# A macaron transformer kernel: the routing of its MoE stages done chunk by chunk, their inner values rounded by another engine, and a norm moved to an earlier layer

## The reference, cut to what matters

```python
x = x + 0.5 * ffn(norm(x))        # L0 FFN, first time
x = x + mamba(norm(x))
x = x + 0.5 * ffn(norm(x))        # L0 FFN, second time
x = x + 0.5 * moe(norm(x))        # L1 MoE, first time
x = x + attention(norm(x))        # 32 heads in all, 1024 x 1024 scores each
x = x + 0.5 * moe(norm(x))        # L1 MoE, second time

def ffn(x):                       # 128 -> 512 -> 512 -> 512 -> 128
    h = silu(x @ w1.T * s1) * (x @ w2.T * s2)
    h = gelu(h @ h1.T * sh1); h = gelu(h @ h2.T * sh2)
    return h @ w3.T * s3

def moe(x):                       # 16 experts of 64 inner values, 4 chosen per token, one shared expert
    scores = sigmoid(x @ gate_w.T)
    idx = top_k(scores + gate_b, 4)
    w = scores[idx] / sum(scores[idx]) * 2.5
    comb[token, idx] = w
    y = sum_e comb[:, e] * (silu_and_mul(x @ w13_e.T) @ w2_e.T)
    return y + silu_and_mul(x @ w13_s.T) @ w2_s.T
```

## Time and profile before

| | |
|---|---|
| median of three executions | 2157.31 us |
| the profiled execution | 2159.68 us, span 2158.4 us |
| PE busy | 1964.8 us, 91% of the span |
| DVE busy | 1332.5 us, 62% |
| POOL busy | 1163.6 us, 54% |
| ACT busy | 1081.9 us, 50% |
| mean granted TensorE clock | 0.945 of full speed |

### The profile page before, as it was taken

How to read it: one execution, slowest core, us unless ns; L and a number is a source line. 1 busy time by engine, 2 the same in 40 slices (tenths; PEclk the granted TensorE clock), 3 DMA queues, 4 the chain that set the end, 5 groups by cost and what they waited for, 6 DMA issues and landing times. The chain is left out here.

```text
span 2158.4 us, 21996 instructions
## 1 busy us (share of the span) xinstructions
PE 1964.8 (91%) x7432; PEld 1314.0 (61%) x7432; DVE 1332.5 (62%) x2243; ACT 1081.9 (50%) x1508; POOL 1163.6 (54%) x632
## 2 busy tenths in 40 slices
PE   6997899897998894799999999999999999998499
PEld 4772333332776562577777777777777777775265
DVE  5326778887344763466576666666666666665466
ACT  4327566554334224465565656555565555553421
POOL 2350547653543443157666675766666666668234
PEclk8998799899998996899999999999999999999689
DMA  2000000000001003231313222231313222200100
GB/s 86 1 1 1 0 0 1 0 0 0 1 1 38 0 6 78 62 67 36 72 42 67 46 62 62 46 72 37 72 37 72 46 62 61 45 11 11 43 6 15
DMA packets 45761, 73.80 MB, mean 34 GB/s; under 512 B 26800, under 2 KB 28400, under 8 KB 45392
## 3 DMA queue, kind: packets, MB, share of 16 engines
q1 hardware_dynamic: 43584, 71.70, 14.4%
q10 hardware_dynamic: 2032, 0.69, 0.1%
q0 software_dynamic: 32, 0.00, 0.0%
HBM read 20.20 MB, written 1.18 MB: 10 GB/s over the span
## 5 line engine op out<-in xcount | busy, mean ns | idle before, releaser
L1883 POOL TENSOR_TENSOR at_e_lo<-at_e,at_e_hi 128x1024 fp32r<-128x1024 f32 x256 | 614.6, 2401 | 395.3 <-DVE at_e_hi L1856 392.8
L1711 ACT ACTIVATE at_e<-at_ps 128x1024 f32<-128x1024 f32 x256 | 263.0, 1027 | 314.9 <-PE at_ps L1618 314.9
L1703 ACT ACTIVATE at_ps<-at_ps,at_neg_diag 128x1024 f32<-128x1024 f32 x256 | 278.6, 1088 | 117.4 <-DVE at_neg_diag L1771 117.4
L1778 DVE TENSOR_REDUCE at_row_max<-at_ps 128x1 f32<-128x1024 f32 x256 | 311.2, 1215 | 15.8 <-PE at_ps L1597 12.7
L1771 DVE CUSTOM_DVE_ANT_0 at_junk_diag<-at_ps,ident 128x128 bf16<-128x128 f32 x256 | 74.6, 292 | 322.8 <-PE at_ps L1570 322.8
L915 POOL TENSOR_TENSOR mb_work<-mb_work,mb_c 128x1024 f32<-128x1024 f32 x64 | 151.6, 2368 | 172.1 <-DVE mb_work L891 167.2
L1856 DVE CAST at_e_hi<-at_e 128x1024 fp32r<-128x1024 f32 x256 | 221.0, 863 | 30.4 <-ACT at_e L1711 30.1
L386 POOL TENSOR_TENSOR ffn_lo<-ffn_hid,ffn_hi 128x512 fp32r<-128x512 f32 x96 | 124.2, 1294 | 189.1 <-DVE ffn_hi L313 189.1
L1568 PE MATMUL at_ps<-at_k,at_q 128*128 128x512 f32 x512 | 172.7, 419 | 16.3 <-DMA at_k<-at_qk_lo 14.2
L1597 PE MATMUL at_ps<-at_k,at_q 128*128 128x512 f32 x512 | 174.3, 422 | 11.3 <-DMA at_k<-at_mask_rows 9.3
L1637 PE MATMUL at_pv_ps<-at_e_lo,at_v_hi 128*128 128x512 f32 x512 | 161.2, 396 | 8.2 <-POOL at_e_lo L1883 8.2
(11 more groups left out here) (310 smaller groups left out, 3762.6 us busy)
## 6 DMA issues: line engine op xcount, KB each, us to landing
at_q<-at_qk_hi SPq DMA_DIRECT2D x64, 256.0 KB, 3.9
at_k<-at_qk_hi SPq DMA_DIRECT2D x32, 512.0 KB, 5.9
at_q<-at_qk_lo SPq DMA_DIRECT2D x32, 256.0 KB, 6.5
at_k<-at_qk_lo SPq DMA_DIRECT2D x32, 256.0 KB, 6.3
at_recips<-at_recip_row SPq DMA_DIRECT2D x32, 256.0 KB, 3.5
ffn_h_raw<-in_h SPq DMA_DIRECT2D x2, 1024.0 KB, 8.4
at_head_w_raw<-in_w_qkv SPq DMA_DIRECT2D x32, 64.0 KB, 4.2
x<-in_x SPq DMA_DIRECT2D x4, 256.0 KB, 5.0
```

Of the source, the lines that this page charges most:

```text
L1703: act.eng.activation(ps[:], ps[:], ACT.Exp, scale=SCALE, bias=m.small["neg_diag"][s][:, blk:blk + 1], accum_out=m.small["sums"][s][:, blk: ...
L1711: act.eng.activation(m.e[e % 2][:], slot("turned_scores", h, blk)[:], ACT.Exp, scale=SCALE).then_inc(sem["at_exp"])
L1778: dve.eng.tensor_reduce(m.small["row_max"][h % SLOTS][:, blk:blk + 1], slot("best", h, blk)[:], AX.X, ALU.max).then_inc(sem["at_best_out"])
L1883: pool.eng.tensor_tensor(m.e_lo[e % 3][:], m.e[e % 2][:], m.e_hi[e % 3][:].bitcast(F32), ALU.subtract).then_inc(sem["at_lo"])
```

## The change

There are five parts.

1. FFN: the norm of the second pair moves from layer 1 to layer 0 of the first pair (mean in slot 0, variance in slot 1, ACT's logarithms in slot 1, the finish in slot 3, the split in slot 4).
2. MoE: the router works on one chunk (four tiles). Chunk 0 is routed before the loop; chunk c + 1 is routed amid the experts of chunk c: DVE finds the best four behind group p = 3 and weighs them behind p = 4, PE turns them over in p = 6, and DVE takes the rest in p = 7. The scores of chunks 1 to 3 are one sigmoid in group 2.
3. MoE: the inner values are rounded by ACT (`round_hidden`), one group behind its SiLU, and no longer by DVE.
4. MoE: the turned-over weights and the matrix that spreads them have 128 rows in place of 48; the added rows are zeros.
5. MoE's start: the norm of chunk 0 is finished before ACT turns to the other three. The loads are in an early and a late group with a semaphore each. The rests of the weights and the copy of `pair_rows` go from DVE to POOL. The rest of chunk 0's input goes to DVE, and those of chunks 1 to 3 stay on POOL but are taken between its first groups.

```diff
@@ ffn_pe (ffn_act and ffn_dve move in the same way)
-                    if layer == 1 and first + 2 < NCH and slot == 0:
+                    if layer == 0 and first + 2 < NCH and slot == 0:
...
-                    if layer == 1 and first + 2 < NCH and slot == 3:
+                    if layer == 0 and first + 2 < NCH and slot == 1:
@@ ffn_dve
-                    if layer == 1 and first + 2 < NCH and slot == 5:
+                    if layer == 0 and first + 2 < NCH and slot == 3:
...
-                    if layer == 1 and first + 2 < NCH and slot == 6:
+                    if layer == 0 and first + 2 < NCH and slot == 4:
@@ moe_pe
+    def turn(ch):
+        pe.wait_ge(sem["moe_route"], MOE_ROUTE * (NCH * t + ch + 1))
...
+        for i in range(CT):
+            mm = pe.eng.transpose(m.banks[ch % 2][:, i * P:(i + 1) * P], m.comb[:, ch * CT + i, :], c.ident[:])
+        mm.then_inc(sem["moe_turned"])
...
+    logits(0)
     expert_in(0)
     expert_in(1)
...
+    logits(1)
+    logits(2)
+    turn(0)
+    logits(3)
     for g in range(MOE_G):
         if g >= 2:
             expert_in(g)
         if g % (PAIRS + 1) < PAIRS:
             spread(g)
+        if (ch := moe_turn_due(g)) is not None:
+            turn(ch)
@@ moe_act
+    for g in range(MOE_G):
+        if g >= 2:
+            silu(g)
+        if g >= 1:
+            round_hidden(g - 1)
+        if g == MOE_SCORES_AT:
+            act.wait_ge(sem["moe_logits"], NCH * (t + 1))
+            act.eng.activation(m.scores_flat[:, CT * EXPERTS:], m.logits_ps[1][:, CT * EXPERTS:],
+                               ACT.Sigmoid).then_inc(sem["moe_scores"])
+        if (ch := moe_turn_due(g)) is not None:
+            turned_out(ch)
@@ moe_dve
-        dve.eng.tensor_copy(m.hid[g % 5][0][rows, :], prod).then_inc(sem["moe_hi"])
         if p == 1 and ch:
             add_out(ch - 1)
+        if p == MOE_ROUTE_AT and ch + 1 < NCH:
+            find_top(ch + 1)
+        if p == MOE_ROUTE_AT + 1 and ch + 1 < NCH:
+            weigh(ch + 1)
+        if p == MOE_TURN_AT + 1 and ch + 1 < NCH:
+            rest_of_turned(ch + 1)
@@ moe
-        m.comb = sb("moe_comb", [P, TILES, REST + EXPERTS])
-        m.comb_t = sb("moe_comb_t", [REST + EXPERTS, TOK], F32R)
-        m.pair_rows = sb("moe_pair_rows_r", [REST + EXPERTS, PAIRS, P], F32R)
+        m.comb = sb("moe_comb", [P, TILES, P])
+        m.comb_t = sb("moe_comb_t", [P, TOK], F32R)
+        m.pair_rows = sb("moe_pair_rows_r", [P, PAIRS, P], F32R)
```

More of the change, by code:

```diff
@@ L289, in ffn_act @@
                     slot = m * 2 + j
-                    if layer == 1 and first + 2 < NCH and slot == 2:
+                    if layer == 0 and first + 2 < NCH and slot == 0:
                         for i in range(2):
                             norm_square(act, c, n0 + first + 2 + i, m_.xn[i], m_.inv[i])
-                    if layer == 1 and first + 2 < NCH and slot == 4:
+                    if layer == 0 and first + 2 < NCH and slot == 1:
                         load_logs(act)
@@ L356, in ffn_dve @@
                     slot = m * 2 + j
-                    if layer == 1 and first + 2 < NCH and slot == 1:
+                    if layer == 0 and first + 2 < NCH and slot == 0:
                         for i in range(2):
@@ L1003, in moe_bank_free @@
     if take < 0:
+        if take >= -4:
+            pe.wait_ge(c.sem["norm_done"], 3 * (8 + 8 * t + take + 4) + 1)
         return
@@ L1023, in moe_bank_free, with moe_turn_due @@
             pe.wait_ge(c.sem["moe_prod"], g0 + g + 1)
+def moe_turn_due(g):
+    ch, p = divmod(g, PAIRS + 1)
+    return ch + 1 if p == MOE_TURN_AT and ch + 1 < NCH else None
 def moe_pe(c, m, t):
@@ L1032, in moe_pe, with logits @@
         norm_variance(pe, c, n0 + ch, m.banks[4 + ch], m.inv[ch])
[L1033 to L1038, removed]
+    def logits(ch):
+        pe.wait_ge(sem["moe_load"], 16 * len(MOE_EARLY_LOADS) * (t + 1))
+        pe.wait_ge(sem["norm_done"], 3 * (n0 + ch) + 3)
+        for i in range(ch * CT, (ch + 1) * CT):
+            mm = pe.eng.matmul(m.logits_ps[min(ch, 1)][:, i * EXPERTS:(i + 1) * EXPERTS], m.xn[:, i * P:(i + 1) * P],
+                               m.loads["gate_w"][:], start=True, stop=True)
+        mm.then_inc(sem["moe_logits"])
     def expert_in(g):
@@ L1134, in moe_dve, with finish @@
     g0 = t * MOE_G
-    dve.eng.memset(m.comb[:], 0.0).then_inc(sem["moe_start"])
-    for ch in range(NCH):
-        norm_centre(dve, c, n0 + ch, m.banks[ch], c.x[:, COLS[ch]], m.xn[:, COLS[ch]])
-    for ch in range(NCH):
+    route = sem["moe_route"]
+    def finish(ch):
         norm_finish(dve, c, n0 + ch, m.banks[4 + ch], m.xn[:, COLS[ch]], m.inv[ch], m.sq[ch])
-    dve.wait_ge(sem["moe_load"], 16 * len(MOE_LOADS) * (t + 1))
-    dve.eng.tensor_copy(m.pair_rows[:], m.loads["pair_rows"][:]).then_inc(sem["moe_start"])
@@ L1188, in add_out @@
         dve.eng.tensor_tensor(c.x[:, COLS[ch]], c.x[:, COLS[ch]], m.banks[ch % 2], ALU.add).then_inc(sem["x_moe"])
+    for ch in range(NCH):
+        norm_centre(dve, c, n0 + ch, m.banks[ch], c.x[:, COLS[ch]], m.xn[:, COLS[ch]])
+    dve.eng.memset(m.comb[:], 0.0).then_inc(sem["moe_start"])
+    finish(0)
+    dve.wait_ge(sem["moe_xn_hi"], NCH * t + 1)
+    dve.eng.tensor_tensor(m.xn_lo[:, COLS[0]], m.xn[:, COLS[0]], m.xn_hi[:, COLS[0]].bitcast(F32),
+                          ALU.subtract).then_inc(sem["moe_first_xn_lo"])
+    finish(1)
+    finish(2)
+    find_top(0)
+    weigh(0)
+    finish(3)
+    rest_of_turned(0)
     for g in range(MOE_G):
@@ L2070, in laid_out @@
     pick = np.tile(np.eye(2 * STATES, dtype=np.float32), (2, 1))
[L2071 removed]
+    pair_rows = np.zeros((P, PAIRS, P), np.float32)
     for p in range(PAIRS):
```

213 lines of the change are left out of this document (128 added, 85 removed).

## The result

The changed kernel takes 2129.76 us in the median of its four runs (2125.9 to 2133.69) against 2156.53 of the kernel before in the same session (2155.01 to 2166.3); the ratio is 0.9867, 95% interval 0.983 to 0.9903. Forecast were 2114 us and a range up to 2129, so the median lies at the very end of that range, 0.8 above it (by the ratio, 0.9867 x 2157.31 = 2128.6, just inside). The profiled execution took 2125.9 us, 33.8 less than that of before (2159.7), where the sum of the terms had said 43.6. So the direction holds, and some 10 us of the gain are missing. The other 6 between 2130 and 2114 come from comparing medians: the profiled execution after is the fastest of its four, that of before was above its median.

What follows compares the result with a forecast made beforehand. PE, busy 91%, was taken to bound the kernel. FFN's 12.2 plus two MoE stages at 15.7 gave 43.6 off 2159.7, 2116.1; less 2.4 for the median, 2113.7, rounded to 2114 us, range 2101 to 2129.

Steps and rivals of the forecast that it cites:

- FFN's norm: w3 of each FFN's first pair: wait and low clock go, gain 6.1 per FFN, 12.2 us in all; bounds 4.5 to 6.3 each.
- nothing is late by more than some tenths: FFN's layers 0 and 1: with the norm moved, GELUs and rests come at most some tenths of a us late.
- 128 rows: MoE loop's spread matmul: group falls from 2.70 to 2.31 us, 23 x 0.39 = 9.0 per stage; bounds 0 and 9.0.
- The rival that the rows don't cost that: MoE spread matmul: gaps at 48 rows have another cause, 18 us are not gained, 2132 us; chance 6%.
- Transposes: PE in the MoE loop: 12 added transposes at 0.23 us cost 2.7 per stage.
- The routing charge: MoE loop: DVE's router takes 3.1 us per chunk; lateness charged 0.3 per chunk, 1.0 per stage, bounds 0 and 3.
- The start: Each MoE ahead of its first spread matmul: 10.6 us gained, bounds 7 and 13, with POOL's operations delaying DVE.
- The first four groups: MoE, first spread to fourth down product: 12.2 us against 12.1 before, no gain and no loss.
- The chain: MoE group's SiLU, product, ACT rounding and POOL rest: 0.4 us of slack before the down product, costing nothing.
- The tail: Very end of each MoE stage: the bare chain has ACT's rounding of 0.6 for 0.43, costing 0.2 us.
- The clock: First groups of the MoE stages: left as it was, one of two stages hit again; none or both, 4 us less or more.
- DVE late at p = 5, on time at p = 7: MoE loop's routing: DVE comes 1.4 us late at p = 5 and is on time again at p = 7.

Runs made afterwards that it cites:

- e4: Kernel before with only FFN's norm moved and 128 rows for 48; start, routing and rounding as before: 2134.56 us, ratio 0.9849.
- e5: Changed kernel with each chunk's routing in four parts behind groups p = 3 to 6, transposes at p = 7: 2123.31 us, ratio 0.9827.
- e7: Changed kernel with the cast of the 128x16 positions done as a tensor_reduce over one element: 2119.29 us.
- e3: Changed kernel with the rests of the first two expert weights made by DVE in place of POOL: 2122.43 us, ratio 0.9808.
- e10: e9 with 16 unread matmuls in PE's wait ahead of the first transposes and 4 ahead of chunk 3's logits: 2119.59 us, ratio 0.9825.
- e9: e6 with the positions turned to f32 by the reduction of e7: 2115.74 us, ratio 0.9814.
- e1: Changed kernel with PE's transposes of the next chunk's routing in group p = 7 in place of 6: 2134.09 us, ratio 0.9865.
- e6: Changed kernel with the four-part routing of e5 and the start of e3 together: 2122.1 us, ratio 0.9792.

## Why the prediction was right or wrong

- **FFN's norm: the wait at w3 went, but the 12.2 is met by luck.** w3 starts at 91.46 with no wait. Yet the two FFNs gain 4.6 and 4.9 us, 9.5 in all, near the lower bound of 4.5 each; the other 2.7 of the 12.2 are Mamba's. The step that failed is "nothing is late by more than some tenths": a PE wait in FFN's layer 1, which I had named as a sign of being wrong, is in both FFNs (0.95 and 0.94), at just the point that I had walked to, where layer 1 first reads the value of slot 6. The timeline of the second FFN has three DVE operations that run long beside POOL ahead of it:

```profile
559.26 1.29 POOL L386 TENSOR_TENSOR ffn_lo<-ffn_hid,ffn_hi 128x512 fp32r<-128x512 f32 x1 [5.96 <-DVE ffn_hi L313]
559.33 1.50 DVE L313 CAST ffn_hi<-ffn_hid 128x512 fp32r<-128x512 f32 x1
561.53 1.23 DVE L156 SCALAR_TENSOR_TENSOR ffn_scratch<-ffn_scratch 128x512 f32<-128x512 f32 x1
566.31 1.67 DVE L308 TENSOR_TENSOR ffn_xn_lo<-ffn_xn,ffn_xn_hi 128x512 fp32r<-128x512 f32 x1
...
572.32 0.50 PE L114 MATMUL ffn_ps<-ffn_hi,h_hi 128*128 128x512 f32 x1 [0.94 <-POOL ffn_lo L386]
```

  POOL's next two rests start at 560.92 and 566.02, each just ahead of the second and the third of these. Elsewhere the three take 0.43, 0.69 and 0.69, so they are 2.6 us longer together. With the longer steps around it the wait costs PE 1.2 us, and 6.1 - 1.2 is the 4.9 measured. No run takes these meetings away, so for FFN their part is argued from the trace and not tested.
- **128 rows: right.** 2.78 per chunk in e4, all three steps at 0.23. The loop of e4's first MoE is 9.9 us shorter for 9.0 forecast. The rival that the rows don't cost that is refuted.
- **Transposes: too dear.** I charged 2.7 per stage for 12. Four of them take PE 0.41 from start to the next matmul, 1.2 per stage. My 0.23 for one was read from transposes that ran at a granted clock of 0.50, as the window over them in the trace of before says:

```profile
706.65:710.26 3.61, 3.61 (x16) 2.43 (x16) 1.56 (x3) 1.77 (x3) 0.00 (x0) 0.50 0.00 0
```

- **The routing charge: this step failed.** "I charge 0.3 per chunk, 1.0 per stage; bounds 0 and 3." Transposes and waits together were to be 1.2 per chunk; e4 and after give 2.67. PE's steps add up to it: 1.50 at the wait for the transposes (1.34 and the longer step), 0.49 for the transposes and the step behind them, 0.66 at the down product's wait. DVE's two parts take 2.8 and 3.1 us, not 1.4 and 1.7, since the cast (1.13 on the mean for 0.17), the product (1.28 for 0.23) and the bias (0.56 for 0.22) stand still beside POOL. I had used exactly this mechanism for the start and did not apply it to the loop, where POOL works 1.29 of every 2.31 us. Three chunks are 4.4 us per stage too much, 8.8 in all; e5 gets them back to 0.97 per chunk, e7 the cast's part alone. The transposes' overcharge hid part of this: the waits alone were charged 0.3 and cost some 2.2 per chunk.
- **The start: right mechanism, one size off.** 28.9 us after the stage's first matmul, 27 forecast; 8.5 gained for 10.6, inside the bounds 7 to 13. The norm step took 2.72, the rest of chunk 0's input 2.07, and the router's cast was caught too (1.88 for 0.17), which I had not foreseen. Its 1.7 us are most of the 2 by which the start came out too long, going by the durations; no run takes it out alone, since in e7 the next operation stood still in its place. e3 shows that taking POOL's first two rests away makes the start 2.0 us shorter.
- **The first four groups: about right, for another reason.** 12.5 us for 12.2. Their clock was 0.50, which I had not forecast for the first MoE; e10 shows that at 1.00 they would be hardly faster (its loop takes 0.35 less than e9's). Against e4 (11.2) it is 1.3 given back.
- **The chain: the claim that 0.4 us of slack costs nothing holds only while DVE is on time.** PE has no wait in the plain groups. But behind a late DVE the slack is gone at once, and PE waits 0.4 for moe_hid_lo after each of the chunk's transposes (e1: up to 1.1). The tail costs 1.42 (1.16 and 0.26) against 0.95 before, 0.5 for the 0.2 forecast.
- **The clock.** The second MoE gained 13.0 and the first 8.5. The difference is about the 4 us that the second had lost before to the low clock in its first groups; now both stages have that clock there, and the second has no more of it than the first. It makes good part of the miss. That, too, is luck: I had left the clock as it was. The sum of what was measured: 9.5 for the FFNs, 2.7 for Mamba, 8.5 and 13.0 for the MoEs are 33.7, and the profiled executions differ by 33.8. Of it 6.7, Mamba's 2.7 and the clock's 4, are not from any term of my sum; my terms gave 27 of their 43.6.
- **DVE late at p = 5, on time at p = 7:** the first half came true, and at p = 6 it was still late by 1.3 to 1.7 us.

The 10.0 us that the loop of the first MoE takes over e4: 3 x 2.67 = 8.0, 1.3 in the first groups, 0.4 in the tail, 0.3 unassigned.

The best version is e9 by its stages, 16.3 and 22.4 us under those of before, and by its median of 2115.74; by the ratio e6 (0.9792) and e9 (0.9814) can't be told apart. Against the change itself (0.9867) the kernels' intervals overlap; it is the stage times, each from one profile, that put e9 7.8 and 9.4 us ahead of it (1.6 of the 9.4 is the clock of the first matmuls).

## What to carry to other kernels

When short VectorE operations are moved out of an idle stretch into a loop in which GpSimd works, price each of them with what GpSimd may have left to run, and put those that read and write SBUF in a copying or two-input form just ahead of GpSimd's start, in pieces that fit; a reduction in their place may pass. A stall that is found at one place of a change must be looked for at every other place where the same pair of engines meets. Run the simple parts of a compound change alone: here they held the whole gain, and what the rest won at the start it lost in the loop. And compare each stage with its own forecast, the stages that didn't change too: a sum that fits can hold a term that doesn't. Look at the granted clock of a row before taking a PE cost from it: the transposes' 0.21 at 0.50 was 0.11 at 1.00.

## What the runs showed of the hardware that was not expected

- A u32 to f32 cast of 128x16 on DVE waits for POOL's operation (1.07 to 1.88 us for 0.17), and so does a one-input f32 tensor_scalar of 128x64 (1.245 for 0.194). tensor_reduce with the same operands took 170 ns in all eight places (e7). MAX8 and FIND_INDEX8 kept their 0.16 to 0.18 us, and the 64 products with one operand in PSUM their means of 0.684 and 0.687, though POOL works more than half of the time there.
- Four transposes of 128x128 take PE 0.41 us from the first's start to the next matmul at a granted clock of 1.00, 0.11 from one to the next, less than half of a 512-column matmul (0.23); at 0.50, in the trace of before, they are 0.21 apart.
- The clock behind the start: in the changed kernel it is 0.50 (the 1.2 GHz level) for the 5.6 us behind the first spread, with PE busy in all of them, after PE had been idle for 4.3 us up to 686.83. In e10, where PE was busy for 6.10 of the 6.86 us ahead, it is 1.00.
